# Token-routed experts: rows sorted by expert through DRAM, one expert per block, in place of all four experts on masked rows

## The reference, cut to what matters

```
tid = clip(token_ids, 0, 12499); e = min(tid // 3125, 3)          # the ids lie in 13..99985
for e in range(4):  y = (silu(h @ ctx[e].T) * (h @ ctx[e].T)) @ ctx[e].T
out = where(expert_ids == e, y, out)                               # h: layer norm of x, ctx: (4, 256, 256)
```

## Time and profile before

| | us |
|---|---|
| median of 3 runs (832.22 to 833.65) | 832.39 |
| profiled execution | 829.35 |
| its span | 827.5 |
| PE busy in the span | 666.7 (81%) |
| DVE busy | 543.0 (66%) |
| ACT busy | 406.8 (49%) |
| POOL busy | 171.5 (21%) |
| granted TensorE clock, mean share of 2.4 GHz | 0.901 |

### The profile page before, as it was taken

One profiled execution on the slowest core, in us unless ns is written; L12 is line 12 of the kernel. 1 busy time (PEld: TensorE's weight loads), 2 busy tenths in 40 slices (PEclk: granted clock), 3 DMA queues, 4 the chain that ended last, 5 costly groups with the idle time before them and its releaser, 6 DMA issues. The chain is left out here.

```text
span 827.5 us, 16974 instructions
## 1 busy us (share of the span) xinstructions
PE 666.7 (81%) x6016; PEld 496.4 (60%) x6016; DVE 543.0 (66%) x1250; ACT 406.8 (49%) x892; POOL 171.5 (21%) x193
## 2 busy tenths in 40 slices
PE   3688887887878889676698798977678887789996
PEld 2345544464667788563466565654456664778996
DVE  5776755366675356683977998867577847864455
ACT  1235444204254345864577567563246646654553
POOL 5100101121400342007032101131411103103213
PEclk9789999999998899988798799897979986899998
DMA  9800000070212351005000000000033101014433
GB/s 298 288 2 2 2 2 2 1 284 1 71 41 75 124 158 40 19 22 135 3 6 7 1 8 6 7 7 2 1 122 119 67 3 41 31 52 154 142 108 116
DMA packets 39070, 53.10 MB, mean 64 GB/s; under 512 B 9874, under 2 KB 33170, under 8 KB 38558
## 3 DMA queue, kind: packets, MB, share of 16 engines
q1 hardware_dynamic: 35918, 43.62, 16.0%
q0 software_dynamic: 3072, 8.39, 3.3%
HBM read 37.97 MB, written 17.04 MB: 66 GB/s over the span
## 5 line engine op out<-in xcount | busy, mean ns | idle before, releaser
L1169 ACT ACTIVATE s_mega<-bank 128x512 f32<-128x512 f32 x96 | 56.0, 598 | 63.8 <-PE bank L1579 41.7
L2157 DVE TENSOR_TENSOR s_mega<-bank,s_mega 128x176 f32<-128x176 f32 x84 | 28.4, 338 | 77.8 <-ACT s_mega L1224 77.6
L2016 DVE TENSOR_REDUCE s_mega<-bank 128x2 f32<-128x512 f32 (+1 forms) x96 | 62.8, 683 | 15.0 <-PE bank L1543 8.7
L2219 DVE SCALAR_TENSOR_TENSOR s_mega<-s_mega,s_convw 128x256 f32<-128x256 f32 x144 | 68.2, 514 | 1.8 <-ACT s_mega L1286 0.8
L2284 DVE TENSOR_TENSOR s_mega<-s_mega 128x512 f32<-128x512 f32 x64 | 47.1, 742 | 13.1 <-ACT s_mega L1379 10.3
L1224 ACT ACTIVATE s_mega<-bank 128x176 f32<-128x176 f32 x84 | 26.8, 319 | 56.0 <-PE bank L1737 55.7
L1022 POOL DMA_INDIRECT xd<-s_xn,s_pos x32 | 33.5, 1047 | 94.7 <-issue 94.7
L1747 PE MATMUL bank<-s_ident,s_mega 128*88 128x128 f32 x168 | 34.9, 292 | 21.5 <-DVE s_mega L2157 21.5
L1387 ACT ACTIVATE s_mega<-bank 128x512 f32<-128x512 f32 x64 | 37.9, 602 | 24.9 <-PE bank L1847 24.6
L1032 POOL DMA_INDIRECT s_mega<-yd,s_pos x32 | 31.7, 989 | 74.9 <-DMA yd<-s_mega 59.7
L968 POOL TENSOR_TENSOR s_rstd<-s_ve,s_mhalf 128x2 f32<-128x2 f32 x24 | 16.8, 698 | 141.5 <-DVE s_ve L1930 129.9
(11 more groups left out here) (278 smaller groups left out, 1948.8 us busy)
## 6 DMA issues: line engine op xcount, KB each, us to landing
s_mega<-xd SPq DMA_DIRECT2D x60, 128.0 KB, 2.1
yd<-s_mega SPq DMA_DIRECT2D x60, 128.0 KB, 1.7
s_wrawF<-in_wF SPq DMA_DIRECT2D x10, 608.0 KB, 5.3
s_wrawC<-in_wC SPq DMA_DIRECT2D x9, 608.0 KB, 10.2
xd<-in_zeros SPq DMA_DIRECT2D x2, 1920.0 KB, 18.2
s_mega<-in_win SPq DMA_DIRECT2D x1, 2112.0 KB, 9.8
s_mega<-in_hots SPq DMA_DIRECT2D x2, 704.0 KB
s_x<-in_x SPq DMA_DIRECT2D x4, 256.0 KB, 4.6
```

The costliest lines, as they stand in the source:

```text
L1169: a.activation(PT[:, p % NPT, :], AR[n % 3][:, :], ACT.Exp).then_inc(a_read, 1)
L2016: v.tensor_reduce(nM[:, q, h0:h0 + heads], W[n % 3][:, :].rearrange("p (h k) -> p h k", h=heads), AX.X, ALU.max, negate=True).then_inc(w_r ...
L2219: ins = v.scalar_tensor_tensor(o, raw[:, m % NRAW, h, KS - 1 - k:KS - 1 - k + L], convw[:, ct, KS - 1 - k:KS - k], o, ALU.mult, ALU.add)
```

## The change: what it does, and the diff

The ids are loaded as an 8-column tile (one row per partition) in place of 1024 broadcast columns, and five small DVE operations make a 0/1 table of the experts. In stage A, steps "b_rank" and "b_route" of each half (five small matmuls; one DVE copy and 13 DVE operations of the same chain as "route", for four experts) give each row a position among the 7 x 128 rows of a half, sorted by expert and padded per expert to whole blocks, and the weight offset of each block. After the layer norm of a batch, "b_send" writes its two tiles of rows to DRAM with indirect DMAs. A block j then runs b_ld (SP load), b_x (PE transposes, ACT copy), b_h (PE product with the expert that a register selects, ACT silu), b_mul (DVE), b_t (PE transposes, ACT copy), b_y (PE product, ACT copy), b_st (SP store). "b_gath" (POOL) brings a tile's rows back and "b_add" (DVE) adds them to x. Each kind of product has one PSUM bank. The "lt" steps of stage B go. Four of C's weight units are loaded in stage A and split in half 0, two more in half 1, three in C. Two more DRAM buffers of 896 rows are zeroed at the start. The new line `max` / `min` clips ids that the masks before took as they were.

```diff
+NBB = (HALF + E0 * (P - 1)) // P
+NB_ALL = 2 * NBB
+NRB, NGB_B = 3, 4
 UNITS = {s: NE + n for s, n in SHARED.items()}
-SPLITS = {"C": (8, 4, 5, 6, 7, 0, 1, 2, 3), "F": (8, 9, 2, 3, 4, 5, 6, 7, 0, 1)}
-SPLIT_EARLY = {"C": 5, "F": 4}
+SPLITS = {"C": (3, 4, 5, 6, 8, 7, 0, 1, 2), "F": (8, 9, 2, 3, 4, 5, 6, 7, 0, 1)}
+SPLIT_EARLY = {"C": 6, "F": 4}
+SHARED_SPLITS = {"C": 5, "F": 2}
+LOADS_IN_A = (0, 1, 2, 3)
...
     def norm(s, b):
         if after[s] is not None:
             steps.append(("ln", after[s], b))
+            if after[s] == "B":
+                steps.append(("b_send", "B", b))
...
     def turn(s, b):
-        if s is not None and s != "E":
+        if s is not None and s not in "BE":
             steps.append(("lt", s, b))
+
+    def b_open(hf):
+        j0 = NBB * hf
+        steps.extend(("b_ld", "B", j0 + j) for j in range(5))
+        steps.extend(("b_x", "B", j0 + j) for j in range(2))
+
+    def b_step(hf, q):
+        def put(kind, j):
+            if 0 <= j < NBB:
+                steps.append((kind, "B", NBB * hf + j))
+
+        put("b_h", q)
+        put("b_mul", q - 1)
+        put("b_t", q - 1)
+        put("b_x", q + 2)
+        put("b_y", q - 2)
+        put("b_ld", q + 5)
+        put("b_st", q - 2)
...
                         turn(nxt, b - 1)
-                    if nxt == "B" and (b, k) == (3, 1):
-                        steps.append(("b_mask", nxt, 0))
+                    if nxt == "B" and b == 0 and k in (5, 9):
+                        steps.extend(((kind, "B", k // 9) for kind in ("b_rank", "b_route")))
+                    if nxt == "B" and (b, k) == (1, 0):
+                        steps.extend(("wload", "C", i) for i in LOADS_IN_A)
...
-                    steps.append(("b_h", nxt, (0, 0)))
+                    b_open(0)
+                    b_step(0, 0)
                 if b + 2 < B:
                     steps.append(("stack_t", s, b + 2))
                 if b + 2 != B:
                     steps.append(("y_t", s, (b, 1)))
                 if nxt == "B" and b == 3:
-                    steps.append(("b_h", nxt, (0, 1)))
+                    b_step(0, 1)
             steps.append(("o_t", s, B - 1))
+            if nxt == "B":
+                b_step(0, 2)
             steps.append(("o", s, B - 1))
             if s == "A":
                 norm(s, B - 1)
...
+            late.clear()
+            b_step(0, 3)
+            steps.extend(("wload", nxt, i) for i in (4, 5))
+            for q in range(4, NBB + 2):
+                b_step(0, q)
+                if q - 4 in LOADS_IN_A:
+                    steps.append(("wsplit", nxt, q - 4))
+            steps.extend(("b_gath", s, t) for t in range(TH))
+            b_open(1)
+            for q in range(NBB + 2):
+                b_step(1, q)
+                if q == 0:
+                    steps.extend(("b_add", s, t) for t in range(NT))
+                    norm(s, 0)
+                if q == 1:
+                    steps.extend(("b_add", s, t) for t in range(NT, TH))
+                    norm(s, 1)
+                    turn(nxt, 0)
+                    steps.extend(("wload", nxt, i) for i in range(6, UNITS["C"]))
+                if q == 2:
+                    turn(nxt, 1)
+                    steps.append(("gate", nxt, 0))
+                if q == 3:
+                    steps.extend((("rank", nxt, 0), ("route", nxt, 0), ("send", nxt, 0)))
+                if q in (4, 6):
+                    steps.append(("wsplit", nxt, 4 + (q - 4) // 2))
+            steps.extend(("b_gath", s, t) for t in range(TH, 2 * TH))
+            steps.extend(("b_add", s, t) for t in range(TH, 2 * TH))
         elif s in "CF":
             bl = blocks(s)
...
+                elif kind == "b_ld":
+                    hf, j = divmod(i, NBB)
+                    if j == 0:
+                        for b in (2 * hf, 2 * hf + 1):
+                            sp.wait_ge(b_sent[b], 16 * NT)
+                    if i >= NRB:
+                        sp.wait_ge(b_x_full, i - NRB + 1)
+                    sp.dma_start(b_rows[i % NRB], xd_b[hf][j * P:(j + 1) * P, :]).then_inc(b_rows_in[i % NRB], 16)
+                elif kind == "b_st":
+                    hf, j = divmod(i, NBB)
+                    sp.wait_ge(b_yb_ready, i + 1)
+                    sp.dma_start(yd_b[hf][j * P:(j + 1) * P, :], b_yb[i % 2]).then_inc(b_y_out[i % 2], 16)
...
+                elif kind == "b_send":
+                    hf = i // 2
+                    if i == 0:
+                        pool.wait_ge(b_zero, 32)
+                    pool.wait_ge(b_pos_ready, hf + 1)
+                    pool.wait_ge(xn_ready, ln_index(s, i) + 1)
+                    for t in range(NT):
+                        g.indirect_dma_start(xd_b[hf], bass.IndirectOffsetOnAxis(b_pos[:, NT * i + t:NT * i + t + 1], 0),
+                                             xn[:, i % 2, t, :], None).then_inc(b_sent[i], 16)
+                elif kind == "b_gath":
+                    hf, t = divmod(i, TH)
+                    if t == 0:
+                        for slot in range(2):
+                            pool.wait_ge(b_y_out[slot], 16 * sum(j % 2 == slot for j in range(NBB * (hf + 1))))
+                    if i >= NGB_B:
+                        pool.wait_ge(b_moved, i - NGB_B + 1)
+                    g.indirect_dma_start(b_got[i % NGB_B], None, yd_b[hf],
+                                         bass.IndirectOffsetOnAxis(b_pos[:, i:i + 1], 0)).then_inc(b_g_in[i % NGB_B], 16)
...
+                elif kind == "b_x":
+                    act.wait_ge(b_x_full, i + 1)
+
+                    if i >= 2:
+                        act.wait_ge(b_h_full, i - 1)
+                    a.copy(b_xT[i % 2], B_X[:, 0:2 * P]).then_inc(b_xT_ready, 1)
                 elif kind == "b_h":
-                    n = at["G"]["b_h", s, *i]
-                    act.wait_ge(g_full, n + 1)
-                    if n >= 2:
-                        act.wait_ge(g_read, n - 1)
-                    a.activation(sg[:, n % 2, :], GB[n % 2][:, :], ACT.Silu).then_inc(s_ready, 1)
+                    act.wait_ge(b_h_full, i + 1)
+
+                    if i >= 2:
+                        act.wait_ge(b_t_full, i - 1)
+                    a.activation(b_act[i % 2], B_H[:, 0:D], ACT.Silu).then_inc(b_silu_ready, 1)
+                elif kind == "b_t":
+                    act.wait_ge(b_t_full, i + 1)
+                    if i >= 2:
+                        act.wait_ge(b_y_full, i - 1)
+                    a.copy(b_aT[i % 2], B_T[:, 0:2 * P]).then_inc(b_aT_ready, 1)
+                elif kind == "b_y":
+                    act.wait_ge(b_y_full, i + 1)
+                    if i >= 2:
+                        act.wait_ge(b_y_out[i % 2], 16 * (i // 2))
+                    a.copy(b_yb[i % 2], B_Y[:, 0:D]).then_inc(b_yb_ready, 1)
...
+                    if s == "C":
+                        act.wait_ge(*previous("B"))
...
+                    hf, j = divmod(i, NBB)
+                    if i == 0:
+                        pe.wait_ge(ctx_in, 32)
+                    pe.wait_ge(b_pos_ready, hf + 1)
+                    pe.wait_ge(b_xT_ready, i + 1)
+                    if i:
+                        pe.wait_ge(b_act_ready, i)
+                    offsets["B", i % 4] = nc.tensor.value_load(b_eb[0:1, hf, j:j + 1], min_val=0, max_val=(E0 - 1) * KD * D)
+                    for k in range(KD):
+                        ins = mm(B_H[:, 0:D], b_xT[i % 2][:, k * P:(k + 1) * P], mega[:, bass.ds(offsets["B", i % 4] + B_W + k * D, D)],
+                                 start=(k == 0), stop=(k == KD - 1))
+                    ins.then_inc(b_h_full, 1)
+                elif kind == "b_t":
+                    pe.wait_ge(b_act_ready, i + 1)
+                    if i:
+                        pe.wait_ge(b_aT_ready, i)
+                    for k in range(KD):
+                        ins = tr(B_T[:, k * P:(k + 1) * P], b_act[i % 2][:, k * P:(k + 1) * P], ident[:, :])
+                    ins.then_inc(b_t_full, 1)
                 elif kind == "b_y":
-                    hf, b = divmod(i, 2)
-
                     if i == 0:
                         pe.wait_ge(p_read, sum(key[1] == "A" for key in at["P"]))
-                        pe.wait_ge(w_read, sum(key[1] == "A" for key in at["W"]))
-                    pe.wait_ge(hm_dve, DVE_EXPERTS * KD * (hf + 1))
-                    pe.wait_ge(hm_pool, (E0 - DVE_EXPERTS) * KD * (hf + 1))
-                    n = at["Y"][s, i]
-
-                    if n >= 2:
-                        pe.wait_ge(y_read, n - 1)
-                    for t in range(NT):
-                        for e in range(E0):
-                            for k in range(KD):
-                                ins = mm(Y[b][:, t * D:(t + 1) * D], xm[:, 1, e, k, (b * NT + t) * P:(b * NT + t + 1) * P],
-                                         ctxT[:, e, k, :], start=(e == 0 and k == 0), stop=(e == E0 - 1 and k == KD - 1))
-                    ins.then_inc(y_full, 1)
```

(48 more changed lines are left out.)

165 lines of the change are left out of this document (78 added, 87 removed).

## The result

The changed kernel took 881.6 us (median of 4 runs, 875.9 to 886.0) against 833.0: ratio 1.0597, 95% interval 1.0549 to 1.0645. That is 49 us slower where 25 were forecast, and outside the range of 843 to 871. The direction was right, two terms of the sum were far too small.

A forecast was written before the change was run, and what follows sets the result against it. It took a chain through DVE's queue, not PE, to bound the expert stage: 103.8 us at half clock, 89.4 at full, against 75.6; with four fifths of the difference +25.3, so 832.39 + 25.3 = 857.7 us, range 843 to 871.

The forecast's parts named there:

- The bound moves from PE to a chain through DVE's list: Expert stage: each block's first product waits for the previous block's DVE product, queued behind other DVE work; PE no longer bounds.
- Half clock for most of it: Expert stage: gaps put PE at 1.2 GHz; four fifths of the 14.4 us between half and full clock; chance 0.60.
- What a block holds of PE: Expert stage: one block's matmuls and transposes take 1.3 us of PE at full clock, 18 us for all 14.
- The register load at 0.27: Expert stage: 0.27 us from release to weight load in each block; at 0.55, up to 3.9 us more in all.
- the stage's sum: From E to stage C's first low part: 103.8 us at half clock, 89.4 at full, against 75.6 before the change.
- The first segment: Start of the expert stage: from E to the end of b_mul 2, 14.1 us, the attention's last add ending at 10.6.
- E: The instant at which the expert stage starts, 146.51 us in the trace before the change; the sum counts from it.
- Store, gather, landing, norms, adds: Expert stage: store to gather 1.95 us, second gather 1.28 later, landing 3.2, add 0.45, norm 3.1.
- the rival of slow landings: Expert stage: stores and register loads at their upper ends, +36 us, 868 us; chance 0.09.
- Stage A and the rest at 0: Outside the expert stage: no net change; stage A within -2.5 to +2.5 us, stage C 0 within 2.
- What a measurement can tell: Whole kernel time: differences down to about 0.2%, 1.7 us, can be told.
- The faster rival: Expert stage: DVE's order doesn't bind, blocks run at 1.8 us, stage 52 us, -24 us, 808 us; chance 0.09.

The follow-up runs named there:

- e3: Changed kernel with ACT's weight cast moved right behind a block's silu and DVE's low part behind the next b_mul: ratio 1.0346, 20.9 us less.
- e4: Changed kernel with half 1's adds moved into stage C's steps 3 and 4: ratio 1.0517, stage 113.8 us, 7.7 less.
- e5: Changed kernel with the first product alternating between two banks from block 3 on: ratio 1.0406, 15.9 us less.
- e8: Changed kernel with useless matmuls added ahead of five waiting products and ahead of stage C: ratio 1.0487, 9.2 us less.
- e6: Changed kernel with both products of a block run over half their contraction, so its output is wrong: ratio 1.0517, stage 108.7 us.
- e1: Changed kernel with each block's register load issued ahead of the wait for the product before it: ratio 1.0502, 7.9 us less.
- e7: Changed kernel with the edits of e1, e3, e4 and e5 together: ratio 1.0083, 43 us less.
- e11: The later e10 but with half 0's adds from step 10, and the last norm, half 1's transposes and some weight loads and splits moved: ratio 1.0002.
- the later e10: e7 with half 1's table in stage A's third batch, half 1's blocks straight behind half 0's, half 0's adds from step 11: ratio 1.0068.

## Why the prediction was right and wrong

- *The bound moves from PE to a chain through DVE's list*: right, shown by the waits and by e3, e4 and e5, which change order, place and one bank and no work, and are worth 21, 8 and 16 us (e4's by its stage, as its time is not clear of the interval).
- *Half clock for most of it*: right (0.67 in the stage; e8).
- *What a block holds of PE* ("4 x 0.22 + 4 x 0.11 = 1.3 us"): wrong, and the largest error. The row of the kernel before has 16 instructions for one group of `b_h`, and the code has 8 matmuls there: each of these calls on four-byte data shows as two instructions (a transpose, in the earlier trace rows, as one). I took the duration of an instruction from the trace and the count of the added ones from the code. The added products are four instructions each, not two: 2.07 us at half clock where the sum has 1.07. A block holds 8 x 0.22 + 4 x 0.11 = 2.2 us of PE at full clock, and the 14 first products alone were busy 24.4 us. Setting the count back to the forecast one (e6) took 12.8 us or more off the stage in its profile.
- *The register load at 0.27*: wrong. The row taken for the release was not one: stage C's list puts the transposes of a block two steps ahead of its product, so the DVE row at 269.74 belongs to a later block. The 0.55 of issue in the same row was the nearer value, and it stood in the text as the upper bound; behind a wait it is 0.89. The Trainium skill (page "DMA: Bandwidth & Descriptors", section "Latency and other measured facts") gives the floor of a `tensor_load` as about 600 ns: the trace agrees, with 0.65 us between a load behind the wait and one ahead of it (e1), if a `value_load` is such a load, which no row names. My reading of the row was wrong.
- *Together*: the stage's sum was taken at 100.9 (75.6 + 25.3) and measured 121.5. e1 (5.7) and e6 (12.8) account for 18.5 of the 20.6 if the two add up, which no run with both shows. The first segment fits: the attention's last add ends 13.2 us after E in e1 and 12.9 in e6, against 14.5 to 16.0 in the profiles in which that stretch is as in the change.
- *Store, gather, landing, norms, adds*: right within 0.4 us each, so the rival of slow landings fell.
- *Stage A and the rest at 0*: stage A lost 1.8 to 3.4 us in nine of ten profiles, mostly 2.8 and so just outside the bounds of 2.5 (cause open), and came out 1.8 earlier in the first; what follows the stage lost 1 to 1.6.
- *The range*: its upper end held slow landings and slow register loads, but no error of a count, which no row had called unknown. What a measurement can tell was too small as well: the result's interval is 0.5% to either side, not 0.2%.
- *The faster rival*: with e3's order and e5's second bank a block step does take 2 to 3 us where nothing else stands in it, and the stage gets shorter than before, by 1.4 to 4.5 us in e7, e11 and the later e10, not by 24; the routing and the gathers keep the rest.

## What to carry to other kernels

Count instructions where the duration is counted: if the trace shows two rows for one call of the code, an added call is two rows too. Where a change replaces matmuls by a chain over four engines, add up one full circle of the chain first, and look in each engine's list for what stands ahead of the link that closes it: here a cast and a low part that nothing needed yet were worth 21 us. A register load, and whatever else does not need what the wait brings, goes ahead of the wait.

## What the runs showed that I had not expected

Work without use made the kernel faster: 16 us more of PE took 9.2 us off the time (e8), as it kept the granted clock at 0.86 in place of 0.67. The prediction held nothing of the kind; the expectation of e8 did. And the same stage A ended anywhere from 144.8 to 149.9 us in profiles of kernels that have it in common, so the window of the stage, which repeated within 1 us (121.5 and 122.4), told edits apart that the whole time did not.
